# Reordering the first turn of layer 1: sigmoids, gates, norms' scratch, and the next group's rows and taps

## What is computed

```python
xc = silu(conv1d(x, conv_w, 4 taps, causal, per channel) + conv_b)
q = _l2n((x @ Wq.T).reshape(B, T, 16, 16))
k = _l2n((x @ Wk.T).reshape(B, T, 16, 16))
v = _ln((x @ Wv.T).reshape(B, T, 16, 16), vn_g, vn_b)
i_gate = sigmoid(xc @ ig_w.T + ig_b)
a = broadcast(sigmoid(xc @ gamma_w.T + gamma_b))
mem = scan over t of  m[t] = a[t] * m[t-1] + i_gate[t] * k[t] * v[t]
o = _ln(_ln(mem, mn_g, mn_b) * q) * gn_g + gn_b          # the outer norm per head
attn = (o * sigmoid(xc @ og_w.T + og_b)) @ Wo.T
ffn = bitlinear(sigmoid(bitlinear(x, w1)) * bitlinear(x, w2), w3)   # ternary weights, 704 hidden
x = x + attn + ffn                                       # x inside is layernorm(x)
```

## Time and profile before

| what | us |
|---|---|
| median of 3 runs (lowest to highest) | 831.69 (831.38 to 834.46) |
| the profiled execution, its own time | 834.6 |
| its span, first to last instruction | 832.6 |
| layer 1's first instruction on ACT (`normalise` of group 0) | 608.4 |
| last matmul group of the first turn begins (`query_key(ahead, 1)` follows `query_key(ahead, 0)` at 652.61) | about 654 |
| first instruction of turn 1 on PE (`b_turn`) | 655.45 |

### The profile page before, as it was taken

The page is one execution under the profiler, slowest core; times in us unless marked ns, Lnnn a source line. Parts: engine busy times, 40 slices in busy tenths (PEclk is TensorE's granted clock), DMA queues, the critical chain, the costliest instruction groups (busy, mean ns, idle before and its releaser), DMA issues. The chain is left out here.

```text
span 832.6 us, 15164 instructions
## 1 busy us (share of the span) xinstructions
PE 740.0 (89%) x5602; PEld 636.9 (76%) x5602; DVE 623.2 (75%) x1095; ACT 467.6 (56%) x746; POOL 424.4 (51%) x369
## 2 busy tenths in 40 slices
PE   3268799999999999999999999999977899999873
PEld 2256678888888888888888888888866677877773
DVE  6989878787687776767768777767346698999965
ACT  4246646655665665665566556657676656665410
POOL 2344354354346567757634524445627386584732
PEclk9569999999999999999999999999989999999985
DMA  5111121112011010101100000020110000000000
GB/s 159 29 40 40 39 78 37 36 48 59 2 33 33 24 46 21 48 27 40 34 3 21 20 3 21 4 96 3 58 35 0 1 1 26 1 1 26 1 26 25
DMA packets 22108, 25.89 MB, mean 31 GB/s; under 512 B 4498, under 2 KB 17170, under 8 KB 22036
## 3 DMA queue, kind: packets, MB, share of 16 engines
q1 hardware_dynamic: 22036, 24.93, 10.5%
HBM read 14.83 MB, written 3.28 MB: 22 GB/s over the span
## 5 line engine op out<-in xcount | busy, mean ns | idle before, releaser
L652 DVE TENSOR_REDUCE neg_max<-s_pair 128x4 f32<-128x1024 f32 x127 | 155.0, 1220 | 75.6 <-PE s_pair L866 75.3
L474 ACT ACTIVATE probs<-t_pair 128x1024 f32<-128x1024 f32 x128 | 131.2, 1025 | 136.4 <-PE t_pair L891 136.1
L371 POOL TENSOR_TENSOR hid<-g,hid 128x512 f32<-128x512 f32 x64 | 82.1, 1282 | 177.9 <-DVE g L763 144.8
L365 POOL TENSOR_TENSOR hid_lo<-hid,hid_hi 128x512 fp32r<-128x512 f32 x64 | 85.5, 1335 | 82.9 <-ACT hid_hi L497 82.8
L866 PE MATMUL s_pair<-K,Q 96*128 96x256 f32 x508 | 85.0, 291 | 15.6 <-DVE neg_max L652 9.3
L866 PEld LDWEIGHTS s_pair<-K,Q 96*128 96x128 f32 x508 | 75.8, 195 | 24.2 <-issue 8.1
L891 PE MATMUL t_pair<-Q,K 104*128 104x512 f32 x256 | 86.2, 418 | 0.3 <-DMA Q<-max_parts 0.3
L933 PE MATMUL down<-hi,hid_hi 128*128 128x256 f32 x256 | 83.9, 328 | 0.8 <-POOL hid_lo L365 0.8
L906 PE MATMUL misc<-probs,V 128*32 128x256 f32 x1024 | 69.4, 389 | 3.4 <-DVE kc L608 2.6
L933 PE MATMUL down<-lo,hid_hi 128*128 128x256 f32 x256 | 71.5, 279 | 0.0
L933 PE MATMUL down<-hi,hid_lo 128*128 128x256 f32 x256 | 71.2, 278 | 0.0
(11 more groups left out here) (260 smaller groups left out, 1956.2 us busy)
## 6 DMA issues: line engine op xcount, KB each, us to landing
stage<-in_ternary SPq DMA_DIRECT2D x18, 256.0 KB, 2.8
Q<-q_hi SPq DMA_DIRECT2D x64, 64.0 KB, 2.0
stage<-in_scales SPq DMA_DIRECT2D x8, 384.0 KB, 3.4
X<-in_x SPq DMA_DIRECT2D x8, 256.0 KB, 4.2
Q<-q_lo SPq DMA_DIRECT2D x32, 64.0 KB, 2.0
Q<-max_parts SPq DMA_DIRECT2D x128, 4.0 KB
out<-X SPq DMA_DIRECT2D x8, 256.0 KB, 2.1
signs<-w_stage SPq DMA_DIRECT2D x9, 128.0 KB, 1.8
```

The costliest lines, as they stand in the source:

```text
L365: pool.tensor_tensor(hid_lo[:, m % 2, :, :].rearrange("p a n -> p (a n)"), hid[:, m % 2, :], hid_hi[:, m % 2, :, :].rearrange("p a n -> p ...
L371: pool.tensor_tensor(hid[:, m % 2, :], g[:, m % 2, :], hid[:, m % 2, :], ALU.mult).then_inc(S["hid_done"], 1)
L474: act.activation(probs[:, u % 2, th, :], t_pair[:], ACT.Exp, scale=SCALE).then_inc(S["probs_done"], 1)
L652: dve.tensor_reduce(neg_max[:, u % 2, 4 * jp:4 * jp + 4], score_banks(u, jp)[:].rearrange("p (s n) -> p s n", n=SEQ), AX_X, ALU.max, negat ...
```

## The change

All of it is in layer 1, nearly all in the first turn.

- PE: `gate(0)` goes between `ffn_up(0)` and `ffn_up(1)`, `gate(1)` and `gate(2)` between `ffn_up(1)` and `ffn_up(2)`; `gamma(1)` and the two `xn_turn(ahead)` go up, before and after `ffn_up(4)`; `gate(3)` goes down, behind `ffn_up(5)`. `gate(1)` of this turn no longer waits for norm_done. `value` and `ffn_up(0)` wait for xn_hi instead of xpad, in every turn.
- ACT: `convolution_gated` goes up, right behind `projected(0)`, and `convolved` before `projected(2)`. `xn_high` is cut in two, `xn_high` and `xn_padded`; for the group ahead `xn_padded` and `first_tap` are done before `hidden(5)`. Gates and hidden steps follow PE's new order.
- DVE: the scratch of `norms` is bank 4 in the first turn; `hidden(1)` stands inside `norms`, after the inverse root, and `hidden(2)` inside `values`, after its second product. Tap 1 of group 1 goes before `hidden(5)`, and tap 2 of group 1 moves from turn 1 to the end of this turn.
- POOL: `hidden_low(4)` goes before `through_input_gate(1)`.

The diff, cut to its core:

```diff
-        def linked(engine, wait, name, steps):
+        def linked(engine, wait, name, steps, between=None):
             for n, step in enumerate(steps):
+                if n == 2 and between:
+                    between()
                 if n:
                     wait(name, n)
...
         def xn_low(engine, g, b):
             wait("xpad_done", b + 1)
+            wait("xn_hi_done", b + 1)
...
# POOL, first turn
                     through_input_gate(pool, early, 0)
                     hidden_low(pool, early, 3)
+                    hidden_low(pool, early, 4)
                     through_input_gate(pool, early, 1)
-                    hidden_low(pool, early, 4)
                     hidden_low(pool, early, 5)
                     xn_low(pool, ahead, 1)
...
# ACT: xn_high(g, b) is cut in two
+                def xn_padded(g, b):
+                    wait = waiter(act, g)
+                    wait("xn_turned", b + 1)
+                    if b == 0:
+                        wait("conv_step", 0)
+                        wait("xn_lo_done0", 0)
+                        wait("xn_lo_done1", 0)
+                    inc(act.activation(xpad[:, :, b, PAD:PAD + SEQ], turned(banks[b][:]), ACT.Copy), "xpad_done")
...
# ACT, first turn
-                    xn_high(early, 0)
-                    xn_high(early, 1)
+                    for b in range(BPG):
+                        xn_high(early, b)
+                        xn_padded(early, b)
                     act.wait_ge(once["loaded"], 16 * N_LOADS)
                     first_tap(early)
                     gate_constants()
                     projected(early, 0)
+                    convolution_gated()
                     projected(early, 1)
                     values_squared(0)
                     values_squared(1)
+                    convolved()
                     projected(early, 2)
                     projected(early, 3)
-                    convolution_gated()
                     sigmoid(0)
                     output_weights()
-                    convolved()
+                    gate(0)
                     hidden_high(0)
-                    hidden(1)
-                    gate(0)
-                    hidden(2)
+                    sigmoid(1)
+                    gate(1)
                     normalise(ahead)
+                    hidden_high(1)
+                    gate(2)
+                    sigmoid(2)
                     decays(0)
-                    gate(1)
                     hidden(3)
-                    gate(2)
-                    gate(3)
+                    decays(1)
+                    xn_padded(ahead, 0)
                     hidden(4)
-                    decays(1)
+                    xn_padded(ahead, 1)
+                    first_tap(ahead)
                     hidden(5)
                     xn_high(ahead, 0)
                     xn_high(ahead, 1)
+                    gate(3)
+                    hidden_high(5)
                     queries_kept()
-                    hidden_high(5)
-                    first_tap(ahead)
                     projected(ahead, 0)
                     projected(ahead, 1)
...
# DVE: norms
-                    inverse_root(flat(ss[:]), banks[3][:, 0:n], flat(sq[:, 0, 0])[:, 0:n], early, 0, "norm_done", banks[3][:, n:2 * n])
+                    scratch = banks[3 if late is not None else 4]
+                    inverse_root(flat(ss[:]), scratch[:, 0:n], flat(sq[:, 0, 0])[:, 0:n], early, 0, "norm_done", scratch[:, n:2 * n])
+                    if between:
+                        between()
...
# DVE, first turn
                     hidden(0)
-                    norms()
-                    hidden(1)
+                    norms(lambda: hidden(1))
                     hidden_low(dve, early, 0)
-                    values(dve, early, 1)
-                    for c in range(2, FFN_CHUNKS):
-                        hidden(c)
+                    values(dve, early, 1, lambda: hidden(2))
+                    hidden(3)
+                    hidden(4)
+                    convolve(ahead, range(1, 2))
+                    hidden(5)
                     xn_low(dve, ahead, 0)
-                    convolve(ahead, range(1, 2))
+                    convolve(ahead, range(2, 3))
                     return
...
# DVE, later turns
                 if early is not None:
-                    convolve(early, range(2, 3))
+                    if late > 0:
+                        convolve(early, range(2, 3))
                     hidden(0)
...
# PE, first turn
                     ffn_up(0)
+                    gate(0)
                     ffn_up(1)
-                    gate(0)
+                    gate(1)
+                    gate(2)
                     ffn_up(2)
                     gamma(0)
-                    gate(1)
                     ffn_up(3)
-                    gate(2)
+                    gamma(1)
+                    xn_turn(ahead, 0)
+                    ffn_up(4)
+                    xn_turn(ahead, 1)
+                    ffn_up(5)
                     gate(3)
-                    ffn_up(4)
-                    gamma(1)
-                    ffn_up(5)
-                    xn_turn(ahead, 0)
-                    xn_turn(ahead, 1)
                     query_key(ahead, 0)
                     query_key(ahead, 1)
```

More of the change, by code:

```diff
@@ L1141, in hidden_low, with values @@
             inc(engine.tensor_tensor(h_lo[:, at, :], hid[:, c % 2, :], h_hi[:, at, :].bitcast(F32), ALU.subtract), f"h_lo_done{c}")
-        def values(engine, early, b):
+        def values(engine, early, b, between=None):
             wait = waiter(engine, early)
@@ L1151, in values @@
                 (heads(k), heads(k), each(ss[:, b, PAIR_HEADS:2 * PAIR_HEADS]), ALU.mult),
-                (k, k, v, ALU.mult)]), f"kv_done{b}")
+                (k, k, v, ALU.mult)], between), f"kv_done{b}")
         def through_input_gate(engine, early, b):
@@ L1310, in xn_high @@
                         wait("up_done", 0)
-                        wait("conv_step", 0)
                         wait("xn_lo_done0", 0)
                         wait("xn_lo_done1", 0)
-                    src = turned(banks[b][:])
-                    inc(act.activation(xn_hi[:, :, SEQ * b:SEQ * b + SEQ], src, ACT.Copy), "xn_hi_done")
-                    inc(act.activation(xpad[:, :, b, PAD:PAD + SEQ], src, ACT.Copy), "xpad_done")
+                    inc(act.activation(xn_hi[:, :, SEQ * b:SEQ * b + SEQ], turned(banks[b][:]), ACT.Copy), "xn_hi_done")
                 def projected(g, t):
@@ L1548, in norms_summed, with norms @@
                         inc(dve.tensor_reduce(ss[:, b, :], sq[:, b, :, :, :].rearrange("p c a (h d) -> p (c a h) d", d=L1_DH), AX_X, ALU.add), "ss_summed")
-                def norms():
+                def norms(between=None):
                     wait = waiter(dve, early)
@@ L1749, in value @@
                     wait = waiter(pe, early)
-                    wait("xpad_done", b + 1)
+                    wait("xn_hi_done", b + 1)
                     wait(f"xn_lo_done{b}", 1)
@@ L1759, in ffn_up @@
                     if c == 0:
-                        wait("xpad_done", BPG)
+                        wait("xn_hi_done", BPG)
                         wait("xn_lo_done0", 1)
@@ L1801, in gate @@
                     wait = waiter(pe, early)
-                    if t == 1:
+                    if t == 1 and late is not None:
                         wait("norm_done", 1)
```

## The result

| | before | after |
|---|---|---|
| median of 7 runs each, us | 831.69 (831.29 to 835.86) | 827.37 (826.08 to 828.46) |
| profiled execution, its own time | 834.6 | 828.4 |
| its span | 832.6 | 826.6 |

The account below looks back on a forecast made before the run. VectorE bounds the kernel from turn 1 on, turns repeating every 46.9 us, so an earlier memory_summed of turn 1 counts in full: 663.4 to 657.8 gains 5.6, giving 826.1 off the median 831.69 (829.0 profiled); range 823.5 to 829.3.

Parts of the forecast that it names:

- the clock rival: PE's 2.8 us idle between gate(3) and query_key(ahead) lowers the clock, costing 1.6; gain 4.0, 827.7 us; chance 0.30.
- the first three parts: First turn: early sigmoids, gates between chunks with scratch in bank 4, hidden steps inside norms and values; 4.3 us won by gate(3).
- the last part: End of first turn: group 1's rows and taps ahead; query_key(ahead, 0) at 649.35, turn 1's ffn_up(0) at 653.0 instead of 657.57.
- Tap 1, input gate and `xn_low(0)`: First turn's end: DVE and POOL take turns, so xn_low(0) ends at 649.3 and query_key(ahead, 0) starts at 649.35.
- the rule of the Trainium skill: Shared SBUF ports are an exclusive lock: a VectorE operation with two SBUF inputs and a GpSimd operation block one another fully.
- the rival without collisions: DVE's and POOL's operations in the first turn's end fall beside each other; gain 7.4, 824.3 us; chance 0.20.
- Tap 2 in turn 1: Without tap 2 in turn 1, memory_summed follows ffn_up(0) by 4.8 us instead of 5.8.
- The low clock: First turn, after PE's wait of 3.03: ffn_up(1) took 3.43 us at clock 0.50, 1.6 more than its like.
- the 8.5 lost: First turn, ffn_up(0) to b_turn: PE has 23.8 us of work in 32.3; waits and a low clock lose 8.5.
- POOL always first: First turn's end: POOL's work, then DVE's, is one row of 10.7 us; gain about 3.7, 828.0 us; chance 0.08.
- slower: Clock stays at 1.2 GHz from the gap at 646.6 through turn 1's projections; 838.1 us; chance 0.06.

Follow-up runs that it names:

- e4: Changed kernel with ACT's convolution_gated and convolved back in their old places; first ffn_up(0) to turn 1's memory_summed 41.57 us, against 33.68 for the changed kernel.
- e3: Changed kernel with the norms' scratch back in bank 3 and gate(1) waiting for norm_done; first ffn_up(0) to turn 1's memory_summed 37.83 us, against 33.68.
- e5: Changed kernel with hidden(1) behind all of norms and hidden(2) behind all of values; first ffn_up(0) to turn 1's memory_summed 35.11 us, against 33.68.
- e2: Changed kernel with group 1's taps 1 and 2 cut to 2 of 256 columns; first ffn_up(0) to turn 1's memory_summed 33.05 us, against 33.68.
- e1: Changed kernel with group 1's tap 2 back in turn 1; first ffn_up(0) to turn 1's memory_summed 33.18 us, against 33.68; ratio to before 0.9922.
- e9: Changed kernel with group 1's transposes, copies and taps back in their old places; first ffn_up(0) to turn 1's memory_summed 36.63 us, against 33.68.
- e6: Kernel before the change with 12 unused matmuls between ffn_up(0) and ffn_up(1); first ffn_up(0) to turn 1's memory_summed 40.23 us, against 40.16.
- e7: Changed kernel with POOL's xn_low(1) before through_input_gate(1) and hidden_low(5); first ffn_up(0) to turn 1's memory_summed 32.45 us, against 33.68.
- f2: Changed kernel with POOL's xn_low(1) before its last input gate, timed on another chip; median 824.88 us, ratio to before 0.9893.
- f3: Changed kernel with POOL's xn_low(1) before its last input gate and turn 1's tap 3 before hidden(0); median 825.14 us, ratio to before 0.9894.

## Why the prediction was right, and where not

**The sum.** Forecast for the profiled execution 829.0, measured 828.4; in the stretch 5.6, measured 6.0 (6.48 in F). The median was forecast at 826.1 and came at 827.37. Median against median the gain is 4.3, by the ratio 5.9: the seven runs of before lie in two groups, four from 831.3 to 831.7 and three from 833.5 to 835.9, and the median falls into the lower one, 2.9 below the profiled execution that the chain was laid over. By the median alone the forecast can't be told from the clock rival (827.7), and 827.37 is only just past the 827.5 from which the prediction called it faster; it is the profile that decides between them.

**The steps**, counted from `ffn_up(0)`, forecast and measured: `ffn_up(1)` 3.8 and 3.72; `ffn_up(2)` 9.0 and 8.94; `ffn_up(3)` 12.9 and 12.66; `ffn_up(4)` 16.6 and 16.46; `ffn_up(5)` 20.0 and 19.97; `gate(3)` 21.8 and 21.91. The table load fell where it was forecast, and the clock stayed up. So the first three parts were right in mechanism and size, and e4, e3 and e5 show that the new order needs each of them: undone alone the sigmoids cost 7.89, the scratch 4.15, the hidden steps 1.43, and the last part 2.95. The four add up to 16.4 and not to 6.5: each undone part leaves a queue that waits for it, while the others are laid out for its presence.

**Tap 1, input gate and `xn_low(0)`** was the step that was mis-sized. `query_key(ahead, 0)` was forecast 26.2 behind `ffn_up(0)` and came at 24.2; PE idled 0.5 there and not 2.8, so that the clock rival had no gap to begin in. The mechanism was right (e2), as the rule of the Trainium skill has it (SBUF — State Buffer, Who interferes with whom), and so was the exception, which the page has too: `hidden(5)`, which reads one input from PSUM, took 0.69 at 646.40 in the midst of POOL's 1.70 from 645.50. The order of the arrivals was wrong. I let POOL take its turn between the two taps; DVE's timeline shows both in 1.70, and then `xn_low(0)` all but unheld:

```profile
644.33 1.70 DVE L1552 SCALAR_TENSOR_TENSOR shared<-xpad,conv,shared 128x512 f32<-128x512 f32 x2 [0.76 <-ACT shared L1306]
646.40 0.69 DVE L1587 TENSOR_TENSOR l_hid<-sig,lbank 128x512 f32<-128x512 f32 x1 [0.37 <-ACT sig L1351]
647.01 0.74 DVE L1138 TENSOR_TENSOR lo<-xpad,lo 128x512 fp32r<-128x512 f32 x1
647.67 2.44 DVE L1552 SCALAR_TENSOR_TENSOR shared<-xpad,conv,shared 128x512 f32<-128x512 f32 x2
```

POOL's `hidden_low(3)` ended at 644.83, half a us sooner against `ffn_up(0)` than in my chain (I had taken `values` at 5.68, it took 5.46 from 635.60 to 641.06, and more was lost in rounding the steps ahead), and its `hidden_low(4)` had to wait for ACT until 645.50. In that gap the second tap slipped through. The second tap ended 22.4 behind `ffn_up(0)` and not 24.0. `xn_low(0)` then got in ahead of POOL's input gate, which I had put before it, and ended at 24.1 and not 26.1: 2.3 of the 2.8 us of idle time were gone. Tap 2 met POOL's input gate and `hidden_low(5)` (2.44, 1.52 and 1.73), where my chain had it meet `hidden_low(5)` and `xn_low(1)`.

Most of this error didn't reach the time, and that was luck. Turn 1's `ffn_up(0)` needs POOL's `xn_low(1)`, and POOL's chain ended where it was forecast, 28.75 behind `ffn_up(0)` against 28.9. So `b_turn` came 1.9 sooner than forecast (27.0 against 28.9), PE then waited 0.92, and `ffn_up(0)` came at 29.0 against 29.8. Put as a term: the way from the forecast to the rival without collisions was 1.8 us (gains of 5.6 and 7.4), and e2 measures 0.63 for the collisions on the path. Its stretch, 33.05, is near that rival's 32.8. So the term was some three times too large, and that is the larger part of the 0.9 by which F, 33.68, fell below the forecast's 34.6.

**Tap 2 in turn 1** was wrong as a reason, though the steps from `ffn_up(0)` over `hidden(0)` and tap 3 to `memory_summed` came as chained (4.8 forecast, 4.7 measured). I had ascribed the shorter way from `ffn_up(0)` to `memory_summed` (5.8 before, 4.7 after) to the tap's absence. In e1 the tap is back and the way is 4.84. What shortens it is that tap 1 no longer stands, held by POOL, ahead of the scan: the scan starts 0.2 behind turn 1's `ffn_up(0)` before, 1.3 ahead of it after, 0.7 ahead of it in e1. In e9, where tap 1 stands there again, the scan starts 0.2 behind and the way is 5.77. Nor did the moved tap hold nobody up, as the prediction had it: it held POOL's last operations, for the 0.65 above.

**The low clock** was read as part of the 8.5 lost. It was, on PE, but `ffn_up(2)` didn't feel it (e6). The sum was not touched, since its steps follow DVE's `hidden(1)`.

**The rivals.** The clock rival fell with its gap; the one without collisions is refuted by POOL's rows (1.70, 1.52 and 1.73, and 1.30 in e2), though the gain in F, 6.48, came half way between the forecast's 5.6 and its 7.4; POOL always first and slower didn't come.

## What to carry to other kernels

Where engines have fixed orders, chain each one's queue with measured lengths and write down at each step who is last; that gave six starts within 0.25 us of the trace. Look for the condition that an order rests on before counting parts: with one of them undone, the new order was worse than the old. And a moved operation is free only where both its own engine and the one that it collides with have time: look at the idle time in its old place first, as for tap 2.

## What the runs showed of the hardware

- Where the clock falls, the cost is where the slow products lie: about 1.5 us for some eight products of 512 columns, nothing at all in the kernel before, all of it with bank 3. It fell in waits of 2.52, 3.03 and 6.53 and stayed at 1.00 through 1.47 and 1.10 close together (e6) and through 1.75 (e9).
- From turn 3's `memory_summed` to turn 4's it is 46.1 to 46.5 or 45.0 to 45.3 us, in kernels with the same order there: before 46.38, after 46.41, e1 46.43, e6 44.97, e7 45.20, f2 45.32. The chain of waits has the 24 output products of turn 3 at 5.01 us before and 3.62 in e6. In both the clock falls between 790 and 792, but it is back near 795 in e6 and near 798 before; see the earlier trace rows (0.50 from 792 to 794). These two kernels have the same order there and `memory_summed` of turn 1 at the same time (663.42 and 663.41); of the 2.2 us between their spans 1.4 arise here and 0.8 in the last products of all (5.20 and 4.43). The start of layer 1 (606.5 to 609.8) is the other part of the scatter between runs that the profiles show. Whether POOL's order in e7 to f3 brings the shorter one about (45.2 to 45.3 in 4 of 4 profiles there, 45.0 to 45.3 in 3 of 10 elsewhere) stays open.
